# 3x3 convolutions of a two-block layer by minimal filtering F(2,3) along the rows

## What is computed

```python
t = silu(bn(conv1x1(gn(x), cv1_w)))              # 512 channels; ys = [t[:256], t[256:]]
for i in range(2):                               # the two blocks
    yi = ys[-1]
    z = silu(bn(conv3x3(yi, m_cv1_w[i], pad=1))) # 256 -> 256
    q, k, v = split(conv1x1(z, m_qkv_w[i]))      # 4 heads of 64
    a = softmax(einsum('bhdi,bhdj->bhij', q, k + (rw + rh)) / 8)
    z = einsum('bhij,bhdj->bhid', a, v)
    ys.append(yi + silu(bn(conv1x1(z, m_cv2_w[i]))))
x = x + silu(bn(conv1x1(concat(ys), cv2_w)))     # layer 0
x = x + l1(gn(x))                                # layer 1: a masked, permuted 1x1 convolution
```

## Time and profile before

| | |
|---|---|
| median of 3 runs | 3311.51 us (3309.32 to 3311.64) |
| profiled execution | 3307.56 us, its span 3305.8 us |
| granted TensorE clock, mean | 0.986 |
| TensorE busy | 3055.2 us, 92% |
| VectorE busy | 1818.9 us, 55% |
| ScalarE busy | 1617.1 us, 49% |
| GpSimd busy | 1163.2 us, 35% |
| costliest group | L686, 3456 matmuls of the 3x3 convolutions, 785.3 us busy |
| L1219 | 512 row maxima, 616.5 us busy |

### The profile page before, as it was taken

How to read it: one execution, slowest core, us unless ns; L and a number is a source line. 1 busy time by engine, 2 the same in 40 slices (tenths; PEclk the granted TensorE clock), 3 DMA queues, 4 the chain that set the end, 5 groups by cost and what they waited for, 6 DMA issues and landing times.

```text
span 3305.8 us, 61456 instructions
## 1 busy us (share of the span) xinstructions
PE 3055.2 (92%) x27308; PEld 1564.0 (47%) x27308; DVE 1818.9 (55%) x2419; ACT 1617.1 (49%) x1922; POOL 1163.2 (35%) x864
## 2 busy tenths in 40 slices
PE   3679999999999999999999999999999999999997
PEld 3534544454544545445444545445454454445453
DVE  5636465465654555464654656546554646536463
ACT  1315475173833646255651838337462556518382
POOL 1114461063512462144611635124621446116151
PEclk8889999999999999999999999999999999999998
DMA  4200000100011000100001000110001000000001
GB/s 139 80 26 30 1 30 27 61 21 29 11 42 56 2 30 24 55 30 1 30 26 54 27 30 8 40 60 2 30 23 55 30 1 30 27 26 30 1 8 45
DMA packets 35896, 105.61 MB, mean 32 GB/s; under 512 B 12976, under 2 KB 15024, under 8 KB 32944
## 3 DMA queue, kind: packets, MB, share of 16 engines
q1 hardware_dynamic: 35632, 101.69, 8.6%
HBM read 80.18 MB, written 21.50 MB: 31 GB/s over the span
## 4 chain that ended last, share of the span: by engine, by line
PE 75%; DVE 8%; POOL 6%; ACT 5%; issue 4%; DMA 1%; SPq 0%; POOLq 0%; ACTq 0%; DVEq 0%
PE ps_u L686 44%; PE ps_u L848 13%; PE ps_o L870 4%; PE ps_o L871 3%; PE ps_u L822 3%; PE ps_o L872 3%; DVE row_max L1219 2%; PE ps_u L705 1%; ACT wide L1002 1%; POOL y_pad L1327 1%; POOL xn L1333 1%; ACT ps_u L1002 1%; POOL z L1327 1%; POOL wide L1327 1%; ACT qk L981 1%
## 5 line engine op out<-in xcount | busy, mean ns | idle before, releaser
L686 PE MATMUL ps_u<-y_pad,w_c 128*128 128x512 f16 x3456 | 785.3, 383 | 0.0
L1219 DVE TENSOR_REDUCE row_max<-ps_u 128x2 f32<-128x1024 f32 x512 | 616.5, 1221 | 230.2 <-PE ps_u L822 230.2
L1353 POOL TENSOR_TENSOR probs<-wide,probs 128x1024 f16<-128x1024 f32 x256 | 544.8, 2128 | 166.0 <-ACT probs L1006 154.6
L686 PEld LDWEIGHTS ps_u<-y_pad,w_c 128*128 128x128 f16 x3456 | 329.9, 97 | 420.7 <-issue 17.7
L1023 DVE SCALAR_TENSOR_TENSOR wide<-wide 128x512 f32<-128x512 f32 x256 | 183.4, 719 | 589.2 <-ACT wide L916 587.4
L848 PE MATMUL ps_u<-qk 64*128 64x512 f16 x3072 | 418.6, 378 | 65.6 <-ACT qk L981 26.4
L915 ACT ACTIVATE wide<-ps_u,par_m_t 128x512 f32<-128x512 f32 x128 | 99.3, 776 | 749.3 <-PE ps_u L686 749.3
L870 PEld LDWEIGHTS ps_o<-v_ext,probs 128*128 128x128 f16 x4096 | 375.6, 96 | 143.5 <-issue 122.2
L870 PE MATMUL ps_o<-v_ext,probs 128*128 128x65 f16 x4096 | 431.2, 193 | 0.0
L871 PE MATMUL ps_o<-v_ext,probs 128*128 128x64 f16 x4096 | 429.0, 195 | 0.0
L872 PE MATMUL ps_o<-v_ext,probs 128*128 128x65 f16 x4096 | 426.4, 191 | 0.0
(11 more groups left out here) (185 smaller groups left out, 4101.5 us busy)
## 6 DMA issues: line engine op xcount, KB each, us to landing
w_c<-w_c_dram SPq DMA_DIRECT2D x15, 2304.0 KB, 8.7
xn<-in_x_dram SPq DMA_DIRECT2D x32, 512.0 KB, 6.0
o_nat<-in_x_dram SPq DMA_DIRECT2D x64, 256.0 KB, 2.7
out_dram<-qk SPq DMA_DIRECT2D x32, 512.0 KB, 2.8
w_c_dram<-w_c SPq DMA_DIRECT2D x2, 2304.0 KB, 7.9
qk<-in_L_conv_m_cv_w_dram SPq DMA_DIRECT2D x2, 1152.0 KB, 7.2
probs<-in_L_conv_m_cv_w_dram SPq DMA_DIRECT2D x2, 1152.0 KB, 10.9
probs<-in_L_conv_cv_w_dram SPq DMA_DIRECT2D x2, 1024.0 KB, 12.7
```

The lines of the kernel that those rows point to most:

```text
L686: ins = e.matmul(o, lhsT, rhs, start=start and k == 0, stop=stop and k == len(pairs) - 1)
L1219: e.reduce_max(row_max[:, g % 2, :, it, half], ps_u[:, use.slot:use.slot + 2, :], axis=AX.X).then_inc(*dve_max.up(i, b, g, half, it))
L1353: e.tensor_tensor(p_part(s, 1), wide[:, w.slot, :], p_part(s, 0), ALU.subtract).then_inc(*pool_lo.up("p", i, b, s))
```

## The change

The convolution along a row is computed two outputs at a time from four inputs: for each pair of columns, four "planes" d0-d2, d1+d2, d2-d1, d3-d1 (up to sign, edges from `edge_sign`) are made of the map once, and the weights of a kernel row become g0, (g0+g1+g2)/2, (g0-g1+g2)/2, g2 (the halves are applied at the end). A half map is then 3 x 2 x 4 x 3 = 72 matmuls of 256 columns into four half-bank planes of two banks. Around it:

- `wino` (fp16, high and low, 4 planes of 34 x 16 for two tiles) replaces the padding; all y maps are contiguous (`y_rest`).
- After each cv1 tile with m >= 2 and each m2 tile of block 0 comes `sums` (four VectorE passes into a wide buffer, then two ScalarE casts) and `sums_lo` (two VectorE passes); the convolution waits for those.
- At the end of a half map ScalarE copies plane 2 halved, VectorE forms two mixed planes and adds them to planes 0 and 1, and tanh and the scaled value are then read from SBUF, the latter after the former.
- The convolution takes a pair of banks from its first quarter on, freed by that addition.
- The order changes: k of pair 1 moves behind (1,1); four row maxima instead of seven stand ahead of the end of (1,1), eight instead of five behind it; between cv2 and l1 each norm is followed by a cv1 tile, an out and its lo.
- Setup: 12 instead of 9 blocks per 128 columns of the 3x3 weights, tap sums on GpSimd (`tap_sums`); 3072 KB per fetch.
- `o_nat` holds one half; `normalise` waits for the transposes that read it; x again waits for the transposes of pair 1.
- The two zero matmuls of a group are gone: its first matmul opens each bank (`start=first`).

```diff
     def ends(self, use, work, hold):
         self.clock += work
-        self.free[use.slot] = self.clock + hold
+        for q in (use.slot, use.slot + 1):
+            self.free[q] = self.clock + hold
...
-            use = conv_use[b, m, n] = banks.take(1.9, 50.0, ("act_tile", ("m1", i, b, m, n)))
+            use = conv_use[b, m, n] = banks.take(1.3, 50.0, ("dve_u", ("m1_pairs", i, b, m, n)), pair=True)
...
-        BESIDE = ((), (("q", 1, 0), ("k", 1, 0)), (), ())
-        HALF_1 = ((("v", 0), 1), (("v", 1), 0), (("k", 0, 1), 0), (("v", 2), 2), (("v", 3), 2), (("k", 1, 1), 0))
+        BESIDE = ((), (("q", 1, 0),), (), ())
+        HALF_1 = ((("k", 1, 0), 0), (("v", 0), 2), (("v", 1), 2), (("k", 0, 1), 0), (("v", 2), 2), (("v", 3), 2), (("k", 1, 1), 0))
...
             plan("m2_split", i, b, m, n, w)
+            if b + 1 < NB:
+                plan_sums(i, b + 1, m, n, w)
             yield
             plan("m2_lo", i, b, m, n, w)
+            if b + 1 < NB:
+                plan_sums_lo(i, b + 1, m, n)
...
-            next(maxima)
-            conv_end(1, 1, islice(maxima, 1))
-            next(maxima)
+            conv_end(1, 1)
...
             plan_gn(i, 1, "gn_var")
+            cv1_lo()
             cv1_out()
-            cv1_lo(2)
+            cv1_lo()
             for t in range(CT):
                 norm(t)
-                cv1_tile(t < CT - 1)
-            cv1_out(2)
-            cv1_lo()
+                cv1_tile()
+                cv1_out()
+                cv1_lo()
             cv1_tile()
-            cv1_lo()
-            cv1_out()
-            cv1_tile()
-            cv1_lo()
-            for _ in range(3):
+            for _ in range(2):
                 cv1_out()
                 cv1_lo()
...
-            def conv_rows(b, m, n, rows):
-                return [p for dy in rows for k in range(HT) for dx in range(3)
-                        for p in three(lambda j: w_c3[:, j, k * TAPS + 3 * dy + dx, m * P:(m + 1) * P],
-                                       lambda j: pad_view(b * HT + k, j, n * ROWS + dy, dx, ROWS))]
+            def conv_rows(use, m, n, row, some):
+
+                every = [(k, q, *p) for k in range(HT) for q in range(PLANES)
+                         for p in three(lambda j: w_c3[:, j, k * UNITS + row * PLANES + q, m * P:(m + 1) * P],
+                                        lambda j: wino[:, k, j, q, (n * ROWS + row) * WT:(n * ROWS + row + ROWS) * WT])]
+                per_plane = len(every) // (HT * PLANES)
+                for at in range(len(every))[some]:
+                    k, q, lhsT, rhs = every[at]
+                    first = row == 0 and k == 0 and q % 2 == 0 and at % per_plane == 0
+                    last = row == 2 and k == HT - 1 and q % 2 == 1 and at % per_plane == per_plane - 1
+                    ins = e.matmul(plane(use, q), lhsT, rhs, start=first, stop=last)
+                return ins
...
-                        for bank in range(2):
-                            e.matmul(ps_o[:, bank, 0:4 * (HD + 1)], ident16[:, :], zeros[:, :], start=True, stop=False)
...
-                            e.matmul(o, p_part(s, 0)[:, cols], v_ext[:, jt, h, 0:HD + 1], start=False, stop=False)
+                            first = jt == 0 and it % 2 == 0 and q == 0
+                            e.matmul(o, p_part(s, 0)[:, cols], v_ext[:, jt, h, 0:HD + 1], start=first, stop=False)
...
+                    e.activation(wide[:, w.slot, 0:HALF // 2], plane(use, 2), ACT.Copy, scale=0.5).then_inc(*act_copy.up("m1_mid", i, b, m, n))
+                    silu_halves_of(w, ("m1", i, b, m, n), "m1", b * HT + m)
+                elif kind == "sums":
+                    i, b, k, n, w, w2 = a
+                    e.wait_ge(*dve_u.at("sums", i, b, k, n))
...
+                    src, dst = sums_view(w2), wino_half(k, 0, n)
+                    for h in range(2):
+                        ins = e.activation(dst[:, h], src[:, h], ACT.Copy)
+                    ins.then_inc(*act_cast.up("wino", i, b, k, n))
...
+                    e.tensor_tensor(ends[:, :, 1:W - 1], x[:, :, 2:W], x[:, :, 0:W - 2], ALU.subtract)
+                    e.tensor_tensor(ends[:, :, 0:W:W - 1], x[:, :, 1:W - 1:W - 3], edge_sign[:, :].unsqueeze(1).to_broadcast([P, ROWS, 2]), ALU.mult)
+                    e.tensor_tensor(mids[:, 0], d[:, 0], d[:, 1], ALU.add)
+                    e.tensor_tensor(mids[:, 1], d[:, 1], d[:, 0], ALU.subtract).then_inc(*dve_u.up("sums", i, b, k, n))
+                elif kind == "sums_lo":
+                    i, b, k, n, w2 = a
+                    e.wait_ge(*act_cast.at("wino", i, b, k, n))
+                    src, hi, lo = sums_view(w2), wino_half(k, 0, n), wino_half(k, 1, n)
+                    for h in range(2):
+                        ins = e.tensor_tensor(lo[:, h], src[:, h], hi[:, h], ALU.subtract)
+                    ins.then_inc(*dve_lo.up("wino", i, b, k, n))
...
+                    add, less = wide[:, w.slot, 0:HALF // 2], wide[:, w.slot, HALF // 2:HALF]
+                    e.wait_ge(*act_copy.at("m1_mid", i, b, m, n))
+                    e.scalar_tensor_tensor(less, plane(use, 3), -0.5, add, ALU.mult, ALU.add)
+                    e.scalar_tensor_tensor(add, plane(use, 3), 0.5, add, ALU.mult, ALU.add).then_inc(*dve_u.up("m1_mids", i, b, m, n))
+                    e.wait_ge(*dve_u.now())
+                    e.tensor_tensor(wide[:, w.slot, HALF:HW].rearrange("p (n j) -> p j n", j=2), wide[:, w.slot, 0:HALF].rearrange("p (j n) -> p j n", j=2),
+                                    ps_u[:, use.slot, :].rearrange("p (j n) -> p j n", j=2), ALU.add).then_inc(*dve_u.up("m1_pairs", i, b, m, n))
...
+                        taps = stage[g % 3].rearrange("p (c d x) -> p c d x", d=3, x=3)
+                        both_ends, less = tap_sums[:, g % 2, 0], tap_sums[:, g % 2, 1]
+                        if g >= 3:
+                            e.wait_ge(*u_full.at("w", 4 - g, len(banks_of(GROUPS[4 - g])) - 1))
+                        small(e.tensor_tensor(both_ends, taps[:, :, :, 0], taps[:, :, :, 2], ALU.add), "tap_ends", g)
+                        small(e.tensor_tensor(less, both_ends, taps[:, :, :, 1], ALU.subtract), "tap_less", g)
+                        e.tensor_tensor(both_ends, both_ends, taps[:, :, :, 1], ALU.add).then_inc(*pool_small.up("tap_sums", g))
...
-                    e.wait_ge(*a_full.at("o", i, 1, 0, 1))
+                    e.wait_ge(*a_full.at("o", i, NB - 1, HT - 1, 1))
```

152 lines of the change are left out of this document (100 added, 52 removed).

## The result

The changed kernel takes **3521.2 us** (median; 3518.7 to 3521.8), the kernel before 3310.9 beside it: a ratio of 1.063 (1.062 to 1.065). The profiled execution took 3518.7 us, its span is 3517.0, so 211 us are to be found. The forecast was 3440 with a range of 3290 to 3530: the sign and most places held and the sum of the terms was 81 us short. The range held by 9 us only, at the end that was set by rival 2's time.

A forecast was written before the change was run, and what follows sets the result against it. The prediction held that the engine ending last at each hand-over decides, not busy TensorE: +11 us over 8 images, +89 before l1, +11 its clock, +20 setup and first tiles, +131 in all, about 3440 us, range 3290 to 3530.

The forecast's parts named there:

- rival 2: Idle stretches leave TensorE at half clock, 7.5 us per image, and three bank pairs cost 7 more: 3530 us; chance 0.14.
- TensorE's saving: Convolution half maps: 72 matmuls of 256 columns at 109 ns for 54 of 512, 4.0 us each, 257 us in all.
- the stretch with cv2 and x again: Second half of an image: cv2 on contiguous y_rest saves 2.0 us, fetching x again later costs 1.0, per image.
- rival of weight loads: Convolution: weight loads show behind the short matmuls, 106 us, half absorbed by waits: +53, 3495 us; chance 0.03.
- B: Convolution of block 0, up to the first logits: 6.2 us less per image (-8 to -4).
- Setup: Weight preparation before the first image: more tap blocks and GpSimd's tap sums, +18 us (10 to 28).
- Stage A: Norm to l1, 7 images: l1 starts 12.7 us later behind sums on VectorE, +89 us in all.
- Stage C: End of block 0's attention: ScalarE waits for two tiles' sums, so m2 starts 2.0 us later (0 to +4).
- Stage D: Convolution of block 1: sums delay the last wino part and TensorE idles 7 us; +5.5 us per image (+2 to +9).
- The clock: TensorE at half clock after idling: +1.6 us per norm-to-l1 stage, 11 in all, and +2 per image after both convolutions' idle stretches.
- The edge pass: In each tile's column sums, VectorE's pass over 32 edge elements: 0.11 us.

The follow-up runs named there:

- the edge experiment: Changed kernel with the sums' two edge columns written by two 16-element tensor_scalar passes instead of one 32-element tensor_tensor with a broadcast operand: 3519.9 us, 1.064.
- the last run: Combined kernel with the mean later, block 1's first sums on GpSimd, no convolution quarter ahead of the second m2, 8 unread matmuls instead of 31: 3260.7 us, 0.9823.
- the last two runs: Combined kernel with the mean at steps 25, 27, 29: 3302.2 us, 0.9948; then also GpSimd sums, no quarter ahead of second m2, 8 unread matmuls: 3260.7 us, 0.9823.

## Why the prediction came out 81 us short

- **TensorE's saving: right.** 109 ns as taken from the values' projection; the stretch with cv2 and x again came out at -1.0, -2.0 and +1.0 as summed (in image 2; in three of seven images it is 66.2, +0.9, where D is shorter by 0.5 to 0.9). The rival of weight loads is out.
- **B: right,** -6.1 beside -6.2; q at U+29.6 beside U+29.5, logits U+64.1 beside U+64. The last image and the run with moved statistics (58.1) confirm the reason.
- **Setup: right.** The first cv1 starts at 214.93 instead of 193.7: +21, where 18 was taken, and 2 more for the first image's tiles, which did not show (U is +21, too).
- **Stage A: the size right, a part of the reason wrong.** +13.9 beside 12.7 (the terms named up to 963.2 add up to 962.8, so 12.3). I counted the sums as the cause; without any sum l1 still comes 6.4 us late (27.9), and with all norms in one line it comes at 21.5 with the sums in place behind them: norms and tiles take turns through GpSimd. Sums add 7.5. So the total came near although its shares were not those that I counted, which is in part luck.
- **Stage C: mis-sized,** +2.0 taken, +6.7 measured (+5.9 in image 1). The delay of ScalarE was right: its z copy behind the last rounding is at 749.08 before and 799.33 after, 76.9 and 82.5 us behind the first logits, +5.6 where 5.0 was taken. What failed is the step from there to m2: the prediction goes from 5.0 to 2.0 and shows no row for the 3 us won back between. The run behind the values' matmuls of step 31, at 753.10 before and 804.48 after, came 6.8 later. The quarters ahead of it began only behind a wait of 2.09 us for p_lo (VectorE's low part of the exponentials) and ran in part at half clock (granted 0.63), 4.37 us for 24 matmuls instead of 2.8. TensorE before, then after:

```profile
747.66 4.13 PE L686 MATMUL ps_u<-y_pad,w_c 128*128 128x512 f16 x18
753.10 2.15 PE L686 MATMUL ps_u<-y_pad,w_c 128*128 128x512 f16 x9
...
804.48 1.47 PE L731 MATMUL ps_u<-wino,w_c 128*128 128x256 f16 x12
```

  The delay itself comes from the sums: without them C is 83.7, with them on GpSimd 83.4. Two tiles are 2 x (1.77 + 1.21) = 6.0 us of VectorE (819.46 to 821.23 in the rows of the edge experiment, and 1.21 for the two low parts by their pitch), all ahead of the last p_lo. ScalarE's casts of them stand ahead of the exponentials as well; no run has the two engines apart.
- **Stage D: the mechanism right, the size wrong,** +5.5 taken (+7.5 with its clock), +11.1 measured. TensorE's run behind the last wino part starts at M+13.4 (M is 808.05 + 2.59; 12.4 taken) and, at half clock, ends at M+18.7, where T, the end of (0,0), was taken at M+15.0. From there the z copy at T+23 and the second maximum at T+26 came as forecast, and the first logits at T+55 instead of T+53. Of the 5.6 us too few, half clock is 4: 24 matmuls behind the 7.56 wait took 5.28 us instead of 2.8, and q and k behind 3.36 took 4.26 instead of 2.75.
- **The clock: mis-sized.** I took 1.6 for A and 2 for the rest. The five runs above exceed their full-clock time by 2.6, 1.8, 1.6, 2.5 and 1.5, 10 us per image, of which A's alone was worth 21 us when filled. That was half of rival 2 (7.5 us per image), and the measured 3521 lies nearer its 3530 than my 3440. Its other half, the pairs of banks, does not appear as a wait in the places above; no run changes the pairs alone, so a share of theirs is not excluded.
- **The edge pass: mis-sized,** 0.11 taken for what occupies 0.52, in each of 64 tiles. That is 26 us of VectorE, about what its total is over the 2090.

Gaps of A 1.2, its clock 1.0, C 4.7 and D with its clock 3.6 make 10.5 us per image (the clock of C and D is inside their gaps), 74 to 84 us for 7 to 8 images: the 81.

## What to carry to other kernels

Where the relieved engine is not the one that ends last, cheaper matmuls shorten the cover of everything that was hidden beside them: price each stage by what was hidden there, not by the engine's total. The change became a gain (0.982) not by less work but by order and place: next image's work moved to where its engine idles, operands made in the order in which they are needed, some of them on an idle engine, short passes kept clear of GpSimd's long ones. The kernel before was not run with the same moves, so the 0.982 is not the value of the short matmuls alone. After every move look at the next hand-over, since twice here (norms in one line, statistics in attention) a stage paid what another had won.

## What the runs showed of the chip that I had not expected

- VectorE and GpSimd exclude each other on some passes: a 4-element pass with two operands in SBUF lasted 1.93 us beside GpSimd's 2.12, a 32-element one 0.62, GpSimd's copy 1.09 instead of 0.62. A product of 512 elements lasted 2.07 beside the norm's 2.12. Passes that read PSUM beside GpSimd kept their 1.22. The Trainium skill, page "SBUF — State Buffer", section "SBUF: two separate sides", has this as an exclusive lock held for a whole instruction between GpSimd and VectorE's passes with two SBUF inputs; the ends of the short passes above, 0.02 to 0.06 us behind GpSimd's, agree. The 16-element pass of the edge run, with one input, was held in the same way (0.60). I had weighed that page's rule nowhere in the prediction; 0.4 us of it lay in every tile with sums.
- Half clock costs time of its own inside a kernel: filling one wait of 14.3 us with unread matmuls kept the granted clock at 1.00 behind it and gave 21 us over 7 images.
- Half clock also came behind short waits: the 12 matmuls on z at 1136.61 (the row of the last run) lasted 5.28 us instead of 2.75 at a granted clock of 0.50. The four waits of TensorE ahead of them were 0.64, 1.12, 1.02 and 1.66 us; it was busy for 2.5 of the 6.6 us before.
- What stays open: block 1's attention still takes 1.1 to 3.6 us more in the last two runs than 58.3 (in the images that have a next one), by the statistics passes, the late chain or gaps inherited from D; it wasn't tried apart.
